# A one-layer token tower: row maxima split and loaded by half the heads, one pipeline step fewer, GpSimd held in three places

## The chip, the cores and the metric

An engine's name in the profile is PE (TensorE), PEld (its weight loads), DVE (VectorE), ACT (ScalarE), POOL (GpSimd) and SP (SyncE, which issues nearly all DMAs here).

## The reference

32 sequences of 512 tokens go through one layer of width 128, in float32:

```python
h = tok_ref(x)                        # pos + nest[nesting] + seg[segments], times W
h = h + attn_ref(layernorm(h))        # 8 heads of 16, softmax over 512 keys
h = h + ffn_ref(layernorm(h))         # 4 experts: relu(x fc1) loA loB fc2, weighted by a gate

scores = einsum('bshc,bthc->bhst', q, k) * factor
attn = softmax(scores, axis=-1)
ctx = einsum('bhst,bthc->bshc', attn, v)
```

The softmax needs the maximum of each row of scores, of which a sequence has 8 heads x 512 rows.

## The kernel before

The program is a software pipeline written out by hand. A step `t` has 16 slots; in it every engine works on several sequences at once, each at another stage: the token embedding of sequence t+4, the queries and keys of t+4 and their pieces of t+3, the row maxima of t+1 and t+2, the attention of t, the output and gate of t-2, the experts' end of t-3. The tables `PRODUCTS`, `ACT_WORK`, `DVE_WORK`, `POOL_WORK` and `SP_WORK` say what each engine does in which slot, and for which sequence; every engine runs its list in order, so an instruction that waits for a semaphore holds up all behind it. SP's and GpSimd's lists have no slots, only an order.

**Scores twice.** Queries and keys are cut into three bfloat16 pieces by GpSimd ("second", "residual", "third"), stored by SP to a DRAM tensor (`stack_dram`, six DMAs) and read back as stacks of 96 rows, `qstk` and `kstk` (three DMAs each, "stack"). One score product per head and 128 queries, [queries, keys] in the bank `mix`, only serves VectorE's row maximum (`row_max`, 32 a sequence). The second, transposed, [keys, queries] in the ring `sc` of three banks, is exponentiated by ScalarE (`exp`, 32 a sequence); it has 24 further rows, in which the negative maxima, again as three pieces for each of 8 heads, are multiplied by ones of the right head and so subtracted. Before, the 32 maxima of a sequence are cut into pieces at once (`cut_max`, four VectorE operations), turned by four products (`turn_max`), copied by one ScalarE copy (`copy_mT`), and one DMA (`load_max`) spreads them over the stack of all heads.

**One step.** Each slot has two maximum products, one product of another stage (`PRODUCTS`) and two score products; behind every fourth slot stand the value products `pv` (16 records). Maxima of a sequence run from slot `MSTART` = 10 of a step to slot 9 of the next, two steps ahead of its exponentials, which fill slots 0 to 15 of step t. `mix` has four banks that take turns: the second maximum of a slot reuses the bank of the other product of the slot before. The exponentials' sums come out of the value products; SP stores them, loads them back spread out, VectorE inverts them (`invert_den`, slot 7), SP stores and loads the inverses, and GpSimd multiplies (`normalise`).

**The order on SP** in a step, before: the six piece stores with the denominators' DMAs between them, ids, the output, inverses, rstd, the maxima's load, weights, and at the end the six stack loads of sequence t+3.

**The start and end.** Steps run from -5 to 34. In step -2, slot 10, the first maxima start; the first exponentials are in step 0, slot 0; step 31 has the last, and steps 32 to 34 drain.

```python
MSTART = 10
return t + (2 if c >= MSTART else 1), (s_max, TILES, 2 * ((c - MSTART) % SLOTS) + kind // 2 + 1)
```

Of the kernel before, what the change touches and what calls it, by code (L numbers as in the profile page):

```python
# [24 lines left out]
ALU = mybir.AluOpType  # L25
# [16 lines left out]
KROWS = STK + 3 * NH  # L42
# [3 lines left out]
MSTART = 10  # L46
RING, MIX = 3, 4
U = 4
HB, H2 = 5, 2
# [5 lines left out]
    ("project", -2), ("fc1_3", -3), ("embed", 4), ("low", -3), ("none", None), ("xn2T", -2), ("out", -3), ("gates", -2),  # L55
    ("turn_gates", -2), ("fc1_0", -2), ("fc1_1", -2), ("mT", 1), ("q", 4), ("fc1_2", -2), ("k", 4), ("v", 4),
# [4 lines left out]
BEFORE, BEHIND = (3, 7), (11,)  # L61

ACT_WORK = [
    (1, 1, "relu", -3, 3), (4, 0, "qk", 3, 0), (4, 0, "qk", 3, 1), (4, 0, "ctx", -1, 1), (6, 0, "xn2T", -2, 0),
    (8, 0, "gates", -2, 0), (9, 1, "gate_exp", -2, 0), (9, 1, "relu", -2, 0), (10, 1, "relu", -2, 1),
    (12, 0, "rT", 4, 0), (12, 0, "wT", -2, 0), (12, 0, "mT", 1, 0), (12, 1, "ctx", 0, 0), (13, 1, "relu", -2, 2),
    (15, 2, "v", 4, 0),
# [40 lines left out]
def tower(nc, x, posT, catT, consts, ident, tokW, qkvT, qkb, bv, ob, woT, wo_q, gateT, fc1T, loA, loBT, fc2T, out):  # L108
# [7 lines left out]
    with ExitStack() as ctx:  # L116
# [60 lines left out]
        onehot = sb("onehot", [HOT, S], BF16)  # L177
# [11 lines left out]
        vals = sb("vals", [P, U, NT, NH, Q])  # L189
# [81 lines left out]
        s_mTmm, s_mT, s_mrow = sem("s_mTmm"), sem("s_mT"), sem("s_mrow")  # L271
# [45 lines left out]
        def _(sp):  # L317
# [883 lines left out]
```

## Time and profile before

| | us |
|---|---|
| three timed runs | 1127.64, 1130.84 (median), 1141.0 |
| the profiled execution | 1126.86 |
| its span, first to last instruction | 1125.1 |
| mean granted clock | 0.962 |

In a row of the timeline the columns are start, length, engine, line, operation, result<-operands, shapes, count, and in brackets how long the engine stood idle before it and for what. In the rows of stretches each engine has its busy time and, in brackets, its number of instructions. Matmuls overlap in the timeline; the chain of waits counts each once. Starts are us from the first instruction.

### The profile page before, as it was taken

The numbers are of one execution on the slowest core, as the hardware profiler recorded it, in microseconds if no ns is written. First come the engines' busy times: TensorE is split into PE (matmuls) and PEld (weight loads), VectorE is DVE, ScalarE is ACT, GpSimd is POOL, SyncE is SP. The second block draws the span as 40 slices with busy tenths as digits, with TensorE's granted clock in tenths as the row PEclk, the third lists the DMA queues.
The fourth block names the chain that finished last, engine by engine and source line by source line (L and its number), as shares of the span: only waits on it lengthen the run. The fifth ranks groups of instructions, "written<-read, shape, count | busy, mean of one in ns | idle before, by whom it ended". The sixth has DMA issues, their size and how long they took to land.

```text
span 1125.1 us, 20263 instructions
## 1 busy us (share of the span) xinstructions
PE 1040.1 (92%) x6158; PEld 407.9 (36%) x6158; DVE 948.8 (84%) x2442; ACT 807.0 (72%) x1578; POOL 682.1 (61%) x684
## 2 busy tenths in 40 slices
PE   4368999999999999999999999999999999989865
PEld 2112233333434434343433443434343343333322
DVE  7498899999989989899999999999999998887312
ACT  2217787777877788787877778778787777856731
POOL 1855676677666666677666666667766666621231
PEclk9558999999999999999999999999999999999997
DMA  2553645555554445555555545565555554541111
GB/s 74 148 135 89 137 106 135 129 137 127 137 130 124 126 121 130 142 127 134 126 137 126 126 121 132 130 143 126 137 125 137 128 126 113 121 96 36 55 50 32
DMA packets 93530, 132.43 MB, mean 118 GB/s; under 512 B 18205, under 2 KB 69918, under 8 KB 87398
## 3 DMA queue, kind: packets, MB, share of 16 engines
q1 hardware_dynamic: 91872, 129.54, 47.9%
q10 hardware_dynamic: 1550, 1.59, 0.6%
q8 instruction: 50, 0.82, 0.3%
q14 instruction: 58, 0.48, 0.1%
HBM read 89.20 MB, written 35.01 MB: 110 GB/s over the span
## 4 chain that ended last, share of the span: by engine, by line
PE 64%; DVE 16%; DMA 6%; ACT 5%; issue 2%; POOL 1%; SPq 1%; POOLq 0%; ACTq 0%; DVEq 0%
PE pv L737 17%; PE mix L750 15%; PE sc L724 13%; DVE negmax L1025 9%; PE mix L804 7%; DMA den_dram<-ctx_sb 4%; PE mix L787 3%; DVE bn L1015 2%; ACT probs L592 2%; PE mix L809 2%; DVE h L1050 2%; PE mix L825 2%; DMA den<-den_dram 2%; ACT qk L596 1%; PE mix L769 1%
## 5 line engine op out<-in xcount | busy, mean ns | idle before, releaser
L1025 DVE TENSOR_REDUCE negmax<-mix 128x1 f32<-128x512 f32 x1024 | 649.0, 679 | 56.8 <-PE mix L750 56.2
L592 ACT ACTIVATE probs<-sc 128x512 f32<-128x512 f32 x1024 | 556.3, 600 | 118.2 <-PE sc L724 112.0
L724 PE MATMUL sc<-qstk,kstk 120*128 120x512 bf16 x1024 | 364.2, 382 | 5.6 <-ACT probs L592 4.9
L750 PE MATMUL mix<-kstk,qstk 96*128 96x512 bf16 x1024 | 331.7, 395 | 24.6 <-DMA kstk<-stack_dram 7.3
L737 PE MATMUL pv<-probs,vals 128*32 128x512 f32 x2048 | 244.8, 595 | 0.0
L528 POOL TENSOR_TENSOR ctxh<-ctx_sb,rdenb 128x512 f32<-128x512 f32 x64 | 81.0, 1268 | 245.3 <-DMA rdenb<-rden_dram 244.5
L750 PEld LDWEIGHTS mix<-kstk,qstk 96*128 96x128 bf16 x1024 | 89.4, 98 | 266.5 <-DVE negmax L1025 76.1
L724 PEld LDWEIGHTS sc<-qstk,kstk 120*128 120x128 bf16 x1024 | 100.1, 98 | 107.5 <-ACT probs L592 33.4
L804 PE MATMUL mix<-xn2T,fc1T_sb 128*128 128x512 f32 x256 | 138.2, 622 | 0.7 <-ACT hid L646 0.7
L508 POOL TENSOR_TENSOR qk<-qk,rstdb 128x512 f32<-128x512 f32 x64 | 81.1, 1269 | 57.9 <-DMA rstdb<-rstd_dram 53.4
L737 PEld LDWEIGHTS pv<-probs,vals 128*32 128x32 f32 x2048 | 59.1, 109 | 117.4 <-issue 100.1
L646 ACT ACTIVATE hid<-mix 128x512 f32<-128x512 f32 x128 | 76.5, 598 | 31.2 <-PE mix L804 28.7
L502 POOL TENSOR_TENSOR pieces<-qkr,pieces 128x512 bf16<-128x512 f32 x64 | 74.0, 1156 | 8.5
L485 POOL TENSOR_TENSOR pieces<-qk,pieces 128x512 bf16<-128x512 f32 x64 | 74.0, 1156 | 6.6 <-ACT pieces L600 6.6
L479 POOL TENSOR_TENSOR qkr<-qk,pieces 128x512 f32<-128x512 f32 x64 | 74.1, 1159 | 0.0
L460 POOL TENSOR_TENSOR rstd<-ve,minus_half 128x4 f32<-128x4 f32 x64 | 64.9, 1013 | 5.0
L458 POOL TENSOR_TENSOR ve<-mv,eps_sb 128x4 f32<-128x4 f32 x64 | 12.9, 201 | 73.8 <-DVE mv L1021 71.1
L804 PEld LDWEIGHTS mix<-xn2T,fc1T_sb 128*128 128x128 f32 x256 | 43.9, 191 | 36.7 <-DVE negmax L1025 24.7
L605 ACT COPY v<-mix 128x512 f32<-128x512 f32 x32 | 18.8, 586 | 46.8 <-POOL vals L520 39.1
L474 POOL TENSOR_TENSOR hb_sb<-h_sb,obias 128x512 f32<-128x512 f32 x32 | 40.5, 1265 | 15.0 <-DVE h L1050 14.8
L1010 DVE TENSOR_TENSOR qk<-mix,posQK 128x512 f32<-128x512 f32 x64 | 43.4, 679 | 7.1 <-POOL qkr L479 6.6
L1050 DVE TENSOR_TENSOR h<-mix,hb_sb 128x512 f32<-128x512 f32 x32 | 22.1, 692 | 28.6 <-PE mix L787 27.5
(141 smaller groups left out, 1088.5 us busy)
## 6 DMA issues: line engine op xcount, KB each, us to landing
stack_dram<-pieces SPq DMA_DIRECT2D x192, 128.0 KB
rdenb<-rden_dram SPq DMA_DIRECT2D x64, 256.0 KB
qstk<-stack_dram SPq DMA_DIRECT2D x31, 384.0 KB, 6.6
kstk<-stack_dram SPq DMA_DIRECT2D x31, 384.0 KB, 8.8
rstdb<-rstd_dram SPq DMA_DIRECT2D x32, 256.0 KB, 3.4
wrow<-w_dram SPq DMA_DIRECT2D x32, 256.0 KB
out<-out_sb SPq DMA_DIRECT2D x32, 256.0 KB, 2.6
qstk<-stack_dram SPq DMA_DIRECT2D x31, 256.0 KB, 7.0
```

The lines of the kernel that those rows point to most:

```text
L479: pool.tensor_tensor(qkr[:, side, :], qk32[:, side, :], pieces[:, side, 0, :], ALU.subtract).then_inc(s_res0, 1)
L485: pool.tensor_tensor(pieces[:, side, 1, :], qk32[:, side, :], pieces[:, side, 0, :], ALU.subtract).then_inc(s_pc1, 1)
L502: pool.tensor_tensor(pieces[:, side, 2, :], qkr[:, side, :], pieces[:, side, 1, :], ALU.subtract).then_inc(s_pc2, 1)
L508: pool.tensor_tensor(qk32[:, side, :], qk32[:, side, :], rstdb[:], ALU.mult).then_inc(s_scaled, 1)
L528: pool.tensor_tensor(ctxh[:, g, :], ctx_sb[:, u % 2, g, :], rdenb[:, g, :], ALU.mult).then_inc(s_ctxh, 1)
L592: act.activation(probs[:, c % 8, i % 2], sc[:, i % RING], ACT.Exp).then_inc(s_exp, 1)
L646: act.activation(hid[:, e, :], aux(f"fc1_{e}", 1), ACT.Relu).then_inc(s_hid, 1)
L724: pe.matmul(sc[:, i % RING, :], kstk[0:KROWS, u, h, j * P:(j + 1) * P], qstk[0:KROWS, u, h, :], start=True, stop=True).then_inc(s_score, 1)
L737: mm = pe.matmul(pv[Q * i:Q * i + Q, :], vals[:, u, 2 * half + jj, 4 * g + i, :], probs[:, 4 * (r % 2) + i, jj, :], start=(half == 0 and j ...
L750: pe.matmul(max_bank(m), qstk[0:STK, u, h, j * P:(j + 1) * P], kstk[0:STK, u, h, :], start=True, stop=True).then_inc(s_mxmm, 1)
L804: pe.matmul(aux(f"fc1_{e}", 1), fc1T_sb[:, e, :], xn2T[:], start=True, stop=True).then_inc(s_fc1mm, 1)
L1025: dve.tensor_reduce(negmax[:, m // NT, m % NT:m % NT + 1], max_bank(m), AX.X, ALU.max, negate=True).then_inc(s_max, 1)
```

## The change

The maxima are handled by halves, of four heads each. The pieces of a half take 12 rows (`MROWS`), since the same 12 rows serve both halves of the heads, so a score product has 108 rows. `cut_max`, `turn_max`, `copy_mT` and `load_max` exist once for each half: four VectorE operations, four products, four small copies and one DMA each. The maxima of a sequence run from slot 7 of the step before to slot 6 of its own, one step ahead; its exponentials from slot 3 (`SSTART`) of its own to slot 2 of the next. The first half is cut in slot 15 (after 16 maxima) and wanted at slot 3, the second is cut in slot 7 and wanted at slot 11. So everything ahead of it moves one step closer: steps run from -4, stacks have three buffers instead of four, embeddings are three steps ahead instead of four. The v products move from slot 15 to slot 4, the turns of weights and rstd keep slot 11, and VectorE's comparison of ids (`hot`) goes from slot 15 to slot 11, into two buffers.

On SP the first half's load and then the six stack loads of the next sequence stand at the start of a step, the second half's load behind the inverses' stores. GpSimd gets three more waits: before the scaling of queries it waits for the first half's cut, before rstd1 (which now stands before the keys' second piece) for the second half's cut, and before `normalise` for the gate and the ids.

```diff
-KROWS = STK + 3 * NH
+MROWS = 3 * NH // 2
+KROWS = STK + MROWS
-MSTART = 10
+SSTART, MSTART = 3, 7
-U = 4
-HB, H2 = 5, 2
+U, UV = 3, 4
+HB, H2 = 4, 2
...
 DVE_WORK = [
...
+    (6, 1, "moments1", 3, 0), (7, 1, "cut", 0, 1), (7, 1, "finish", -3, 0), (7, 1, "invert_den", -1, 0),
...
+    (13, 0, "add_qk", 3, 0), (15, 1, "cut", 1, 0), (15, 1, "add_qk", 3, 1),
...
 SP_WORK = [
+    ("max_in", 0, 0), ("stack", 1, 0), ("stack", 1, 1),
...
-            def load_max(b, u):
-                upto(sp, s_mT, b)
-                sp.dma_start(qstk[STK:KROWS, u, :, :],
-                             mT[:].unsqueeze(1).broadcast_to([3 * NH, NH, S])).then_inc(s_mrow, 16)
+            def load_max(b, g, u):
+                upto(sp, s_mT, b, 8, 4 * g + 4)
+                sp.dma_start(qstk[STK:KROWS, u, 4 * g:4 * g + 4, :],
+                             mT[:, g].unsqueeze(1).broadcast_to([MROWS, 4, S])).then_inc(s_mrow[g], 16)
...
             def rstd_first(b):
+                upto(pool, s_mp, b - 3, 8, 8)
...
             def scale(b, side):
+                if side == 0:
+                    upto(pool, s_mp, b - 2, 8, 4)
...
+            def normalise(b):
+
+                if b < NSEQ - 1:
+                    upto(pool, s_gate, b - 1, 13)
+                    upto(pool, s_hot, b + 5)
...
-                act.copy(mT[:], aux("mT", 1)[0:3 * NH]).then_inc(s_mT, 1)
...
+                for j in range(NT):
+                    act.copy(mT[:, g, j * P:(j + 1) * P], bank[Q * j:Q * j + MROWS, g * P:g * P + P]).then_inc(s_mT, 1)
...
-                if i == 0:
-                    upto(pe, s_mrow, b, 16)
+                if i % 16 == 0:
+                    upto(pe, s_mrow[g], b, 16)
...
+            def second_half(t):
+
+                if runs(t - 2):
+                    upto(pe, s_gat, t - 2)
+                else:
+                    mix_free(t, 3 * 7 + 1)
+                turn_max(t, 1)
```

SP where one step ends and the next begins, before. `qstk<-mT` is the maxima's load, `qstk<-stack_dram` and `kstk<-stack_dram` the stacks:

```order
L379 DMA qstk<-mT 24x8x512 [waits s_mT]
L375 DMA w_dram<-turned 4x4x128 [waits s_win,s_wT]
L412 DMA rstdb<-rstd_dram 128x512 [waits s_rstdout,s_scaled]
L417 DMA wrow<-w_dram 128x1x512 [waits s_wout,s_low]
L356 DMA qstk<-stack_dram 48x1x4096 [waits s_score,s_pcoutq]
L356 DMA qstk<-stack_dram 32x1x4096
L356 DMA qstk<-stack_dram 16x4096
L363 DMA kstk<-stack_dram 48x4096 [waits s_score,s_pcoutk]
L363 DMA kstk<-stack_dram 32x1x4096
L363 DMA kstk<-stack_dram 16x4096
L339 DMA stack_dram<-pieces 8x16x512 [waits s_stkq,s_pc0]
L339 DMA stack_dram<-pieces 8x16x512 [waits s_stkk,s_pc0]
```

and now:

```order
L376 DMA w_dram<-turned 4x4x128 [waits s_win,s_wT]
L413 DMA rstdb<-rstd_dram 128x512 [waits s_rstdout,s_scaled]
L418 DMA wrow<-w_dram 128x1x512 [waits s_wout,s_low]
L380 DMA qstk<-mT 12x4x512 [waits s_mT]
L357 DMA qstk<-stack_dram 48x1x4096 [waits s_score,s_pcoutq]
L357 DMA qstk<-stack_dram 32x1x4096
L357 DMA qstk<-stack_dram 16x4096
L364 DMA kstk<-stack_dram 48x4096 [waits s_score,s_pcoutk]
L364 DMA kstk<-stack_dram 32x1x4096
L364 DMA kstk<-stack_dram 16x4096
L340 DMA stack_dram<-pieces 8x16x512 [waits s_stkq,s_pc0]
L340 DMA stack_dram<-pieces 8x16x512 [waits s_stkk,s_pc0]
```

The half's load stands between the weights' load and the stacks, so the stacks wait behind it for ScalarE's copies (`s_mT`).

SP in the middle of a step, before. `stack_dram<-pieces` that waits for `s_pc1` is a second piece, `rden_dram<-rden` the inverses' stores, `rdenb` their load:

```order
L422 DMA out<-out_sb 128x4x128 [waits s_out]
L339 DMA stack_dram<-pieces 8x16x512 [waits s_pc1]
L392 DMA rden_dram<-rden 4x16x32 [waits s_rden,s_rdin1,s_rdin0]
L392 DMA rden_dram<-rden 4x16x32
L339 DMA stack_dram<-pieces 8x16x512 [waits s_pc2]
L400 DMA rdenb<-rden_dram 128x1x512 [waits s_rdout,s_ctxh]
L400 DMA rdenb<-rden_dram 128x1x512 [waits s_ctxh]
```

and now:

```order
L423 DMA out<-out_sb 128x4x128 [waits s_out]
L340 DMA stack_dram<-pieces 8x16x512 [waits s_pc1]
L393 DMA rden_dram<-rden 4x16x32 [waits s_rden,s_rdin1,s_rdin0]
L393 DMA rden_dram<-rden 4x16x32
L380 DMA qstk<-mT 12x4x512 [waits s_mT]
L401 DMA rdenb<-rden_dram 128x1x512 [waits s_rdout,s_ctxh]
L401 DMA rdenb<-rden_dram 128x1x512 [waits s_ctxh]
L340 DMA stack_dram<-pieces 8x16x512 [waits s_pc2]
```

The second half's load stands behind the second piece and the inverses' stores, and before the inverses' load; the third piece (`s_pc2`) moved behind that.

GpSimd in the middle of a step, before. `ve` and `rstd` are rstd1's two operations, `pieces<-qk,pieces` a second piece, `qkr` the residual, `pieces<-qkr,pieces` the third piece:

```order
L485 TENSOR_TENSOR pieces<-qk,pieces 128x512 [waits s_pcoutq,s_pc0]
L479 TENSOR_TENSOR qkr<-qk,pieces 128x512 [waits s_pc0]
L502 TENSOR_TENSOR pieces<-qkr,pieces 128x512 [waits s_pcoutq,s_res0,s_pc1]
L485 TENSOR_TENSOR pieces<-qk,pieces 128x512 [waits s_pcoutk,s_pc0]
L458 TENSOR_TENSOR ve<-mv,eps_sb 128x4 [waits s_mv1,s_rTmm,s_v]
L460 TENSOR_TENSOR rstd<-ve,minus_half 128x4 [waits s_ve1]
L479 TENSOR_TENSOR qkr<-qk,pieces 128x512 [waits s_pc0]
L502 TENSOR_TENSOR pieces<-qkr,pieces 128x512 [waits s_pcoutk,s_res0,s_pc1]
L528 TENSOR_TENSOR ctxh<-ctx_sb,rdenb 128x512 [waits s_rdin0]
```

and now:

```order
L487 TENSOR_TENSOR pieces<-qk,pieces 128x512 [waits s_pcoutq,s_pc0]
L481 TENSOR_TENSOR qkr<-qk,pieces 128x512 [waits s_pc0]
L504 TENSOR_TENSOR pieces<-qkr,pieces 128x512 [waits s_pcoutq,s_res0,s_pc1]
L459 TENSOR_TENSOR ve<-mv,eps_sb 128x4 [waits s_rTmm,s_mv1,s_v,s_mp]
L461 TENSOR_TENSOR rstd<-ve,minus_half 128x4 [waits s_ve1]
L487 TENSOR_TENSOR pieces<-qk,pieces 128x512 [waits s_pcoutk,s_pc0]
L481 TENSOR_TENSOR qkr<-qk,pieces 128x512 [waits s_pc0]
L504 TENSOR_TENSOR pieces<-qkr,pieces 128x512 [waits s_pcoutk,s_res0,s_pc1]
L535 TENSOR_TENSOR ctxh<-ctx_sb,rdenb 128x512 [waits s_rdin0,s_hot,s_gate]
```

rstd1 moved in front of the keys' second piece and waits for `s_mp`, the second half's cut; the multiplication by the inverses waits for `s_gate` and `s_hot` as well.

TensorE in slot 7, before. `mix<-kstk,qstk` is a maximum product, `sc` a score product, `mix<-xn2T,gateT_sb` the gate, `pv` the values:

```order
L750 MATMUL mix<-kstk,qstk 128x512 [waits s_xn2T]
L750 MATMUL mix<-kstk,qstk 128x512 [waits s_max]
L724 MATMUL sc<-qstk,kstk 128x512 [waits s_exp] x2
L794 MATMUL mix<-xn2T,gateT_sb 32x128 [waits s_xn2T,s_max]
L794 MATMUL mix<-xn2T,gateT_sb 32x128 x3
L737 MATMUL pv<-probs,vals 32x512 [waits s_ctx,s_exp,s_v]
L737 MATMUL pv<-probs,vals 32x512 x7
L750 MATMUL mix<-kstk,qstk 128x512 [waits s_out]
L750 MATMUL mix<-kstk,qstk 128x512 [waits s_max]
```

and now:

```order
L763 MATMUL mix<-kstk,qstk 128x512 [waits s_xn2T]
L763 MATMUL mix<-kstk,qstk 128x512 [waits s_stkk,s_stkq,s_max]
L737 MATMUL sc<-qstk,kstk 128x512 [waits s_exp] x2
L811 MATMUL mix<-xn2T,gateT_sb 32x128 [waits s_xn2T,s_max]
L811 MATMUL mix<-xn2T,gateT_sb 32x128 x3
L750 MATMUL pv<-probs,vals 32x512 [waits s_ctx,s_exp,s_v]
L750 MATMUL pv<-probs,vals 32x512 x7
L797 MATMUL mix<-id,mpc 12x128 [waits s_mp,s_gat]
L797 MATMUL mix<-id,mpc 12x128 x3
L763 MATMUL mix<-kstk,qstk 128x512 [waits s_out]
L763 MATMUL mix<-kstk,qstk 128x512 [waits s_max]
```

The first maximum product of the slot is now the first of a new sequence and waits for both stacks (`s_stkk`, `s_stkq`); the second half's turn stands behind the values.

## Rows read from the trace of the kernel before

**Rows 1.** Busy times by stretch (us, busy and instruction count by engine, PEclk, DMA share, GB/s).

```profile
49.71:85.83 36.12, 26.11 (x70) 6.19 (x69) 34.48 (x65) 4.94 (x10) 24.24 (x25) 0.50 0.61 143
501.97:533.63 31.66, 31.22 (x193) 12.31 (x192) 28.72 (x76) 25.05 (x50) 21.20 (x21) 1.00 0.54 130
815.02:846.21 31.19, 31.05 (x193) 12.35 (x192) 28.70 (x76) 24.92 (x50) 21.24 (x21) 1.00 0.53 126
1044.43:1070.39 25.96, 23.56 (x144) 9.19 (x144) 5.71 (x26) 20.63 (x43) 6.61 (x8) 1.00 0.17 51
```

**Rows 2.** The chain of waits, 815 to 850 us: start, length, what.

```profile
820.78 0.09 PE mix L780 x2
...
826.18 0.28 PE mix L774 x4
...
826.68 1.85 PE pv L737 x16
...
841.53 0.43 PE mix L750 x2
...
844.47 0.54 PE mix L750 x2
...
845.55 0.43 PE mix L750 x2
...
849.68 0.43 PE sc L724 x2
```

**Rows 3.** ScalarE's timeline in the fill.

```profile
25.05 3.60 ACT L581 CAST kstk<-const_sb 24x4096 bf16<-24x4096 f32 x1
```

**Rows 4.** ScalarE's timeline of a steady step.

```profile
821.45 0.26 ACT L636 COPY turned<-mix 16x128 f32<-16x128 f32 x1
```

**Rows 5.** SP's timeline of the same step.

```profile
823.89 0.87 SPq L379 DMA_DIRECT2D qstk<-mT  x1
...
827.95 1.87 SPq L356 DMA_DIRECT2D qstk<-stack_dram  x3
829.92 1.58 SPq L363 DMA_DIRECT2D kstk<-stack_dram  x3
...
838.56 0.52 SPq L369 DMA_DIRECT2D den_dram<-ctx_sb  x1
...
842.39 0.34 SPq L385 DMA_DIRECT2D den<-den_dram  x1
...
845.08 0.59 SPq L339 DMA_DIRECT2D stack_dram<-pieces  x1
845.78 1.11 SPq L392 DMA_DIRECT2D rden_dram<-rden  x2
```

**Rows 6.** DMA issues, 815 to 847 us: KB each, median us to landing.

```profile
kstk<-stack_dram SPq DMA_DIRECT2D x1, 128.0 KB, 10.1
ids_b<-ids_dram SPq DMA_DIRECT2D x1, 64.0 KB, 2.6
...
den<-den_dram SPq DMA_DIRECT2D x1, 16.0 KB, 1.8
```

**Rows 7.** DMA issues in the fill, 56 to 86 us.

```profile
kstk<-stack_dram SPq DMA_DIRECT2D x2, 128.0 KB, 8.3
```

**Rows 8.** GpSimd's timeline of the steady step.

```profile
821.01 2.52 POOL L528 TENSOR_TENSOR ctxh<-ctx_sb,rdenb 128x512 f32<-128x512 f32 x2 [6.33 <-DMA rdenb<-rden_dram]
...
840.90 1.16 POOL L485 TENSOR_TENSOR pieces<-qk,pieces 128x512 bf16<-128x512 f32 x1
...
843.42 1.16 POOL L479 TENSOR_TENSOR qkr<-qk,pieces 128x512 f32<-128x512 f32 x1
```

**Rows 9.** VectorE's timeline of the steady step.

```profile
817.31 0.19 DVE L1033 CAST mpc<-negmax 128x32 bf16<-128x32 f32 x1
...
818.11 0.68 DVE L1025 TENSOR_REDUCE negmax<-mix 128x1 f32<-128x512 f32 x1
```

**Rows 10.** VectorE's timeline in the fill.

```profile
73.73 0.95 DVE L1033 CAST mpc<-negmax 128x32 bf16<-128x32 f32 x1
```

More of the change, by code:

```diff
@@ L81 @@
-    ("residual", 3, 1), ("third", 3, 1), ("normalise", -1, 0), ("v", 3, 0),
+    ("scale", 2, 0), ("add_bias", 2, 0), ("scale", 2, 1), ("rstd2", -2, 0), ("norm2", -2, 0),
+    ("second", 2, 0), ("residual", 2, 0), ("third", 2, 0), ("rstd1", 3, 0), ("second", 2, 1),
+    ("residual", 2, 1), ("third", 2, 1), ("normalise", -1, 0), ("v", 3, 0),
 ]
 SP_WORK = [
-    ("piece", 3, (0, 0)), ("piece", 3, (1, 0)), ("den_out", -1, 1), ("piece", 3, (0, 1)), ("den_in", -1, 0),
-    ("piece", 3, (0, 2)), ("ids", 5, 0), ("out", -3, 0), ("piece", 3, (1, 1)), ("rden_out", -1, 0), ("piece", 3, (1, 2)),
@@ L86 @@
-    ("rden_in", -1, 0), ("rstd_out", 4, 0), ("den_out", 0, 0), ("max_in", 1, 0), ("weights_out", -2, 0),
-    ("rstd_in", 4, 0), ("weights_in", -2, 0), ("stack", 3, 0), ("stack", 3, 1),
+    ("max_in", 0, 0), ("stack", 1, 0), ("stack", 1, 1),
+    ("piece", 2, (0, 0)), ("piece", 2, (1, 0)), ("den_out", -1, 1), ("piece", 2, (0, 1)), ("den_in", -1, 0),
+    ("piece", 2, (0, 2)), ("ids", 4, 0), ("out", -3, 0), ("piece", 2, (1, 1)), ("rden_out", -1, 0), ("max_in", 0, 1),
+    ("rden_in", -1, 0), ("piece", 2, (1, 2)), ("rstd_out", 3, 0), ("den_out", 0, 0), ("weights_out", -2, 0),
@@ L309, in steps @@
         def steps(eng, step):
-            for t in range(-5, NSEQ + 3):
+            for t in range(-4, NSEQ + 3):
                 step(t, t % U)
@@ L451, in _ @@
         def _(pool):
-            for v in range(U):
+            for v in range(UV):
                 pool.memset(vals[:, v, :, 0:4, HC:Q], 1.0).then_inc(s_pconst, 1)
@@ L635, in copy_wT @@
                 upto(act, s_wout, b - 1, 16 * WREP)
-                act.copy(wT, aux("mT", 1)[Q:Q + NT * NE, 0:P]).then_inc(s_wT, 1)
+                act.copy(wT, aux("turned", 1)[Q:Q + NT * NE, 0:P]).then_inc(s_wT, 1)
             def copy_rT(b):
@@ L662, in step @@
                 for c in range(SLOTS):
-                    if t == -4 and c == 13:
+                    if t == -3 and c == 13:
                         fill_heads()
+                    if t == -3 and c == 4:
+                        copy_rT(0)
                     for place in range(3):
                         for name, ahead, part in [w[2:] for w in ACT_WORK if w[:2] == (c, place)]:
-                            if runs(t + ahead):
+                            if runs(t + ahead) and not (name == "rT" and t == -3):
                                 work[name](t + ahead, (u + ahead) % U, part)
-                        if place < 2 and runs(t):
-                            exp(t, 2 * c + place)
+                        b = t if c >= SSTART else t - 1
+                        if place < 2 and runs(b):
+                            exp(b, 2 * ((c - SSTART) % SLOTS) + place)
             steps(act, step)
@@ L850, in mix_user @@
                     name, ahead = PRODUCTS[c]
-                    if name == "none":
-                        return -1, (s_h, 1, 1)
-                    if name == "mT" and not runs(t + 1):
-                        return (t - 2, (s_wT, 1, 1)) if t > 0 else (t + 4, (s_rT, 1, 1))
+                    if name == "turned":
+                        return (t - 2, (s_wT, 1, 1)) if runs(t - 2) else (t + 3, (s_rT, 1, 1))
+                    if name == "gates" and runs(t):
+                        return t, (s_mT, 8, 8)
                     return t + ahead, products[name][1]
-                return t + (2 if c >= MSTART else 1), (s_max, TILES, 2 * ((c - MSTART) % SLOTS) + kind // 2 + 1)
+                return t + (1 if c >= MSTART else 0), (s_max, TILES, 2 * ((c - MSTART) % SLOTS) + kind // 2 + 1)
             def mix_free(t, n):
@@ L866, in row_tile @@
             def row_tile(t, u, c, i):
-                ahead = 2 if c >= MSTART else 1
+                ahead = 1 if c >= MSTART else 0
                 if runs(t + ahead):
@@ L1106, in tile_max @@
             def tile_max(t, c, i):
-                ahead = 2 if c >= MSTART else 1
+                ahead = 1 if c >= MSTART else 0
                 if runs(t + ahead):
```

181 lines of the change are left out of this document (90 added, 91 removed).

## The prediction, made before the changed kernel ran

> **What bounds the kernel now.** I read the busy times by stretch first, then the chain of waits through one step, then the four other engines' timelines of the same step. In a steady step TensorE is busy 31.05 us of 31.19 at the full 2.4 GHz (granted clock 1.00), VectorE 28.70, ScalarE 24.92, GpSimd 21.24 [rows 1]. A faster neighbour buys almost nothing there: 0.14 us a step. The chain of waits says the same: it is mostly TensorE's own products, one behind the other, from one group of value products to the next [rows 2]. Two stretches are different. Before the first exponential, VectorE's maxima run alone: 36.12 us for 22 slots, 1.64 us a slot, TensorE at granted clock 0.50 (its lower level, 1.2 GHz) [rows 1]. And in the last step with exponentials, which has no maxima, the step takes 25.96 us instead of 31.19 [rows 1], so a slot with maxima costs 0.33 us more than one without.
>
> The profiled execution took 1126.86 us, its span 1125.1, so 1.8 lie around it; the median of the three timed runs is 1130.84. I sum against 1126.86. A difference of about 2% (1108 to 1153 about the median) is what a measurement of this kernel can tell from none.
>
> **The change part by part.** *One pipeline step less.* The maxima of a sequence now start 12 slots before its exponentials, not 22, and the exponentials start at slot 3 of their step. From the first maximum to the start of step 0 it was 22 slots and is 9: 13 x 1.64 = 21.3 us less. Against it: the maxima now also fill step 31 up to slot 6, 13 slots more at 0.33 = 4.3 us. Step 32 gets 6 score products, 6 x 0.22 = 1.3 us (two took 0.43 in the chain [rows 2]). And in the fill ScalarE's head rows (3.60 us [rows 3]), which were written while ScalarE waited, now stand in front of the first query copy: 0 to 3.6, I take 2. Together 21.3 - 4.3 - 1.3 - 2 = 13.7 us gained once.
>
> *TensorE's own work.* Score products have 108 rows instead of 120 but the same 512 columns, so I cost them at nothing. The turn of the maxima becomes 8 products for 4; two took 0.09 us in the chain [rows 2], so +0.18 a step. The v products (0.28 [rows 2]) only move, from slot 15 to slot 4. The value products now follow their exponentials by less than a slot, not by four: in front of those of slot 11 ScalarE will just be finishing. That wait lies beside the load of slot 11 (below), so it costs nothing of its own; without that cover it is about 0.3.
>
> *The stack loads move behind the half's load; the first cover to go.* Let S be the end of the value products in slot 15, 826.68 + 1.85 = 828.53 [rows 2]. The turn takes 0.18, then ScalarE makes four copies; the nearest row is its 16x128 copy, 0.26 [rows 4], so 1.1 with the gaps: 829.9. Then SP issues the half's load (the whole one held SP 0.87 [rows 5]) and only then the six stack loads: 830.4 to 830.8 where the first started at 827.95 [rows 5], so 2.7 later. They were wanted a step later; now slot 7 of the same step wants them all. The last of the six was issued at about 829.92 + 1.58 - 0.6 = 830.9 and landed after 10.1 us [rows 5, 6], at 841.0. Shifted it lands at 843.7; if it lands after 8.3, as in the fill [rows 7], at 841.9. TensorE reaches slot 7's first maximum at 841.53 + 0.22 = 841.75 [rows 2], plus 0.18 for the turn and 0.28 for v: 842.2. So it waits 0 to 1.5 us. Ahead of the loads there is less in the queue than now, but more than in the fill; I take 0.8, the middle. Behind the waiting product stand that slot's scores, gates and values, and everything after.
>
> *The second half.* It is cut in slot 7, turned behind slot 7's values and wanted in slot 11. The turn ends 0.18 after 844.47 [rows 2], the four copies 1.1 after that, 845.8; the second maximum of slot 8 reuses that bank and stood at 845.55 [rows 2], 845.7 with the turn. With semaphores 0 to 0.4, I take 0.2.
>
> *GpSimd held.* "rstd1" now stands ahead of the keys' second piece and waits for the second half's cut. Before, the piece starts at 840.90, rstd1 follows it, and the next piece starts at 843.42 [rows 8]: 2.5 us for the two. Count from T, the start of slot 7's first maximum: product 0.4, maximum 0.68, cut 0.80 (817.31 to 818.11 [rows 9]), so the cut is done at T + 1.9; rstd1 and the piece 2.5, a semaphore 0.1: T + 4.5. For GpSimd this is hidden: it sits idle 6.33 us a step for the denominators anyway [rows 8], and the second hold (gate and ids, in slot 11) ends about when those land. But SP stands in order: the store of this piece, the two denominator stores, and then the second half's load. From 845.08 to 845.78 and 1.11 more [rows 5] is 1.8, so the load starts at T + 6.3. A 64 KB load lands after 2.6 us and a 16 KB one after 1.8 [rows 6]; this one has 48 KB. It lands at T + 8.1 to 8.9, and later if it queues behind the output's store. TensorE wants it at 849.68 - 841.75 = 7.93 [rows 2], plus 0.18 and 0.2: T + 8.3. A wait of 0 to 1.3; I take 0.5.
>
> What the hold buys is the cut itself. In steady steps a cut's first operation takes 0.19 us [rows 9]; with GpSimd busy beside it, in the fill, one took 0.95 [rows 10]. The Trainium skill (SBUF — State Buffer, "Who interferes with whom") says why: VectorE's second port pair and GpSimd's are one, locked for a whole instruction. By that rule the new cut of slot 7, unheld, would lose up to one GpSimd operation, and the hold is worth about 0.8 a step; the trace of the fill agrees with 0.95 against 0.19, but in steady steps of before there is no such loss to win back. My sum has the cut at 0.80 and needs no sentence of this.
>
> *Sum.* Per step 0.18 + 0.8 + 0.2 + 0.5 = 1.68; bounds 0.18 and 0.18 + 1.5 + 0.4 + 1.3 = 3.4. 31 steps have all of it: 52 us (6 to 105). 1126.9 - 13.7 + 52 = **1165**. VectorE's four extra operations (about 0.2 each), ScalarE's eight small copies (8 x 0.26) and the moved v copy lie in those engines' spare 2.5 and 6.3 us.
>
> **Rivals.** *Everything lands in time.* The stack loads take the fill's 8.3 us and the half's load 1.8, so TensorE never waits: 1126.9 - 13.7 + 6 = 1119. For it: a load slower than the fill's has always had other loads ahead of it. Against: 841.9 against 842.2 leaves 0.3 us of room, and only if nothing is late. It decides once the last stack load lands within 11.5 us of the first one's issue.
>
> *The denominators come late too.* Their store was issued at 838.56, behind the stack loads, and the load back only at 842.39 [rows 5]: 3.8 us. With the stacks 2.7 us later VectorE may wait for them in slot 7, where its maxima queue behind, for another 1 us: 1165 + 31 = 1196. The Trainium skill (DMA: Bandwidth & Descriptors, "Queues, rings and completion order") says that each DMA engine takes its descriptors in the order of the ring; by that rule the store must wait for all of the stacks' descriptors on its engines, and the 3.8 us agree. Against this rival: VectorE itself reaches that point 1.5 us later, since the cut and the output's sum now stand in front.
>
> *The steady step gets shorter.* Some steps took 31.66 instead of 31.19 [rows 1]; if that is VectorE waiting for denominators, later demand ends it, and if the loads land as well it is 1119 - 10, about 1108. Nothing else in the rows could give: TensorE has no more than 0.14 us a step to win.
>
> **How the numbers follow.** Waits as summed 0.55, with its own range 1140 to 1190; all in time 0.25; denominators late as well 0.15; steady step shorter 0.05. Below 1108: 0.05 of the last and 0.02 of the second, 0.07. Above 1153: 0.42 of the forecast and 0.15, 0.57. Within 2%: 0.36. The range 1112 to 1196 leaves out about 0.05 below and 0.08 above.
>
> **What would show it.** Right: the first exponential near 70 us instead of 85.8 [rows 1]; steady steps of about 32.9 us; TensorE waiting each step for the stack load at the first maximum of slot 7 and for the maxima's load at the first score of slot 11, with SP's piece store behind GpSimd just before. Wrong: steps of 31.4 or less, or the waits elsewhere, say at slot 3 for the first half. Steps over 34 us, with VectorE's reciprocal waiting for the denominators, would be the second rival.

## The result, and the profile after

The changed kernel takes 1177.16 us (median of 4 runs, 1173.64 to 1178.84) where the kernel before took 1129.24 us beside it: ratio 1.040, 95% interval 1.032 to 1.049. It is slower. The profiled execution took 1178.84 us, its span 1177.0.

First the length of a step. VectorE compares the ids once in each step, so the time from the first to the last start of that group, divided by one less than its count, is the mean step: before (921.4 - 264.0) / 21 = 31.30 us, after (921.0 - 254.5) / 20 = 33.33. The row is from the view of one tile, 250 to 950 us: count, ns least/median/most, first and last start. Of before:

```profile
L996 DVE TENSOR_SCALAR onehot<-ids_b,const_sb x22: 332/382/857, 264.0 to 921.4; 96x512 bf16<-96x512 bf16 x22
```

Of after, with the exponentials of the whole span, whose first start fell from 85.8 [rows 1] to 70.7:

```profile
L1021 DVE TENSOR_SCALAR onehot<-ids_b,const_sb x21: 338/340/342, 254.5 to 921.0; 96x512 bf16<-96x512 bf16 x21
...
L599 ACT ACTIVATE probs<-sc x1024: 589/597/699, 70.7 to 1130.4; 128x512 f32<-128x512 f32 x171
```

So 15.1 us are gained at the start, and 2.03 a step are lost: 31 x 2.03 = 63. Behind the last exponential 3.5 us are gained (1177.0 - 1130.4 = 46.6; before 1125.1 - 1075.0 = 50.1, by the same view). The spans differ by 51.9, so another 7.5 us are lost; they lie in the steps that fill and empty the pipeline, since the steady steps and both ends are counted.

Busy times by stretch of after, the fill from the first maximum to the first exponential and one steady step, which answer to [rows 1]:

```profile
52.77:70.68 17.91, 14.29 (x38) 3.09 (x36) 17.00 (x32) 1.29 (x6) 11.53 (x12) 0.50 0.34 92
827.22:860.24 33.02, 31.24 (x196) 12.63 (x195) 29.90 (x80) 26.30 (x57) 20.94 (x22) 1.00 0.49 120
```

TensorE is still busy 31.24 us and at granted clock 1.00, but now 1.8 us of the step are idle. The four groups of value products cut the step into four parts, which shows where. Before, TensorE's timeline:

```profile
826.61 1.92 PE L737 MATMUL pv<-probs,vals 128*32 128x512 f32 x16
...
835.29 1.90 PE L737 MATMUL pv<-probs,vals 128*32 128x512 f32 x16
...
842.57 1.90 PE L737 MATMUL pv<-probs,vals 128*32 128x512 f32 x16
...
850.04 1.92 PE L737 MATMUL pv<-probs,vals 128*32 128x512 f32 x16
...
857.79 1.92 PE L737 MATMUL pv<-probs,vals 128*32 128x512 f32 x16
```

After, the same, with the only idle times over 0.15 us in the step, which are all that this view shows (in brackets, with what ended them):

```profile
827.22 1.92 PE L750 MATMUL pv<-probs,vals 128*32 128x512 f32 x16
...
829.46 0.23 PE L797 MATMUL mix<-id,mpc 128*12 128x128 bf16 x4 [0.32 <-DVE mpc L1065]
829.99 0.60 PE L763 MATMUL mix<-kstk,qstk 96*128 96x512 bf16 x2 [0.30 <-DVE qk L1035]
...
836.81 1.90 PE L750 MATMUL pv<-probs,vals 128*32 128x512 f32 x16
...
844.43 1.90 PE L750 MATMUL pv<-probs,vals 128*32 128x512 f32 x16
...
847.09 0.38 PE L737 MATMUL sc<-qstk,kstk 108*128 108x512 bf16 x1
847.61 0.61 PE L763 MATMUL mix<-kstk,qstk 96*128 96x512 bf16 x2
...
852.59 0.60 PE L737 MATMUL sc<-qstk,kstk 108*128 108x512 bf16 x2 [0.91 <-DMA qstk<-mT]
853.12 1.92 PE L750 MATMUL pv<-probs,vals 128*32 128x512 f32 x16
...
860.24 1.92 PE L750 MATMUL pv<-probs,vals 128*32 128x512 f32 x16
```

| part of the step | before | after | difference |
|---|---|---|---|
| values of slot 15 to slot 3 | 8.68 | 9.59 | +0.91 |
| slot 3 to 7 | 7.28 | 7.62 | +0.34 |
| slot 7 to 11 | 7.47 | 8.69 | +1.22 |
| slot 11 to 15 | 7.75 | 7.12 | -0.63 |

The last part only lost work: the turn (behind slot 11 before) and the v products, which now stand in slot 4. The second part grew mostly by those v products. So the losses lie in two places, slot 15 and slot 11, with a smaller one in slot 8. Slot 7's stack load, where the prediction put its largest term, is small. TensorE's waits of after, 250 to 950 us (total, times, longest), some 21 steps:

```profile
PE sc L737 <- DMA qstk<-mT: 17.0, 20, 2.0
PE mix L797 <- DVE mpc L1065: 7.8, 19, 0.6
PE mix L763 <- DVE qk L1035: 6.2, 21, 0.3
PE mix L763 <- DMA kstk<-stack_dram: 2.1, 7, 0.5
```

Of the same stretch, a wait of TensorE's weight loads:

```profile
PEld mix L763 <- ACT mT L620: 10.3, 21, 0.5
```

*Slot 8.* The slot's second maximum product starts 0.52 us behind the score product before it (847.09 to 847.61), where it was 0.22 (845.17 to 845.39). It reuses the bank from which ScalarE copies the second half, and the last of those copies ends at 847.56 (below). This loss of 0.30 is in no bracket, because it falls into gaps under 0.15.

*Slot 11.* SP's timeline of that step:

```profile
831.79 2.33 SPq L357 DMA_DIRECT2D qstk<-stack_dram  x3
...
848.14 0.59 SPq L340 DMA_DIRECT2D stack_dram<-pieces  x1
848.85 1.11 SPq L393 DMA_DIRECT2D rden_dram<-rden  x2
850.00 0.87 SPq L380 DMA_DIRECT2D qstk<-mT  x1
```

GpSimd's, of both places:

```profile
827.66 1.18 POOL L524 TENSOR_TENSOR vals<-v,rstd 128x256 f32<-128x256 f32 x2
...
845.70 0.20 POOL L459 TENSOR_TENSOR ve<-mv,eps_sb 128x4 f32<-128x4 f32 x1 [3.25 <-DVE mpc L1065]
...
846.96 1.15 POOL L487 TENSOR_TENSOR pieces<-qk,pieces 128x512 bf16<-128x512 f32 x1
```

and ScalarE's four copies of the second half:

```profile
846.46 1.10 ACT L620 CAST mT<-mix 12x128 bf16<-12x128 f32 x4 [1.14 <-PE mix L797]
```

The half was ready at 847.56 and its load went out at 850.00, 2.4 us later. In between SP stood at the store of a piece, which GpSimd finished at 848.11 because it had been held to 845.70, and then issued that store and the two of the inverses, 1.8 us.

*Slot 15.* VectorE's two cuts (first and second half):

```profile
827.99 0.32 DVE L1059 CAST mpc<-negmax 128x16 bf16<-128x16 f32 x1
828.34 0.55 DVE L1061 TENSOR_TENSOR mres<-negmax,mpc 128x16 f32<-128x16 f32 x1
...
844.81 0.17 DVE L1059 CAST mpc<-negmax 128x16 bf16<-128x16 f32 x1
845.01 0.19 DVE L1061 TENSOR_TENSOR mres<-negmax,mpc 128x16 f32<-128x16 f32 x1
```

The held cut of slot 7 has 0.17 and 0.19. In slot 15 GpSimd's values (827.66 to 828.84) run beside it; the hold that is meant for this cut stands on the scaling of the queries, one place behind the values in GpSimd's order, so the values are free to run into the cut.

### The profile page after: what moved, and what is told of

Read it like the earlier page. It is cut to its first block and busy times, and to the rows that moved or that the text cites. A ratio compares the mean times of both kernels' runs of the same rounds, so it can differ in the third digit from the quotient of the medians.

```text
span 1177.0 us, 21121 instructions
## 1 busy us (share of the span) xinstructions
PE 1049.2 (89%) x6286; PEld 416.8 (35%) x6286; DVE 975.2 (83%) x2570; ACT 852.0 (72%) x1802; POOL 681.7 (58%) x684
## 5 line engine op out<-in xcount | busy, mean ns | idle before, releaser
L599 ACT ACTIVATE probs<-sc 128x512 f32<-128x512 f32 x1024 | 562.6, 605 | 78.9 <-PE sc L737 72.7
L737 PE MATMUL sc<-qstk,kstk 108*128 108x512 bf16 x1024 | 369.1, 384 | 26.4 <-DMA qstk<-mT 24.4
L763 PE MATMUL mix<-kstk,qstk 96*128 96x512 bf16 x1024 | 325.2, 390 | 42.6 <-DVE qk L1035 11.5
L750 PE MATMUL pv<-probs,vals 128*32 128x512 f32 x2048 | 250.8, 608 | 1.4 <-ACT probs L599 0.9
L763 PEld LDWEIGHTS mix<-kstk,qstk 96*128 96x128 bf16 x1024 | 83.2, 98 | 246.5 <-DVE negmax L1050 67.5
L737 PEld LDWEIGHTS sc<-qstk,kstk 108*128 108x128 bf16 x1024 | 97.6, 98 | 148.3 <-ACT probs L599 43.9
L620 ACT CAST mT<-mix 12x128 bf16<-12x128 f32 x256 | 65.7, 257 | 100.1 <-PE mix L797 95.4
L518 POOL TENSOR_TENSOR v<-v,posV 128x512 f32<-128x512 f32 x32 | 40.7, 1273 | 3.9 <-ACT v L612 3.9
```

What stands on the lines that cost most here:

```text
L599: act.activation(probs[:, c % 8, i % 2], sc[:, i % RING], ACT.Exp).then_inc(s_exp, 1)
L737: pe.matmul(sc[:, i % RING, :], kstk[0:KROWS, u, h, j * P:(j + 1) * P], qstk[0:KROWS, u, h, :], start=True, stop=True).then_inc(s_score, 1)
L750: mm = pe.matmul(pv[Q * i:Q * i + Q, :], vals[:, b % UV, 2 * half + jj, 4 * g + i, :], probs[:, 4 * (r % 2) + i, jj, :], start=(half == 0 ...
L763: pe.matmul(max_bank(m), qstk[0:STK, u, h, j * P:(j + 1) * P], kstk[0:STK, u, h, :], start=True, stop=True).then_inc(s_mxmm, 1)
```

## The experiments

All are edits of the changed kernel. "Step" is worked out as above; "cut" and "half's load" are how long TensorE waited, between 250 and 950 us, for VectorE's cut and for the maxima's load, counting waits over 0.15 us.

| run | median us | ratio to before, interval | step | cut (times) | half's load (times) |
|---|---|---|---|---|---|
| the changed kernel | 1177.16 | 1.040, 1.032 to 1.049 | 33.33 | 7.8 (19) | 17.0 (20) |
| e1_rstd1_free | 1197.68 | 1.061, 1.058 to 1.064 | 34.24 | 33.7 (40) | 0.5 (1) |
| e2_half_load_first | 1177.61 | 1.044, 1.040 to 1.047 | 33.66 | 28.6 (21) | none |
| e3_v_in_front | 1163.87 | 1.030, 1.027 to 1.033 | 32.94 | 0.3 (1) | 20.1 (21) |
| e4_both | 1147.99 | 1.017, 1.014 to 1.019 | 32.34 | 9.1 (22) | none |
| e5_v_free | 1149.94 | 1.017, 1.015 to 1.020 | 32.35 | none | none |
| e6_rden_first | 1148.00 | 1.016, 1.014 to 1.018 | 32.36 | none | none |
| e7_no_holds | 1231.39 | 1.090, 1.087 to 1.093 | 34.96 | 41.0 (37) | none |
| e8_stacks_first | 1411.45 | 1.250, 1.245 to 1.255 | 41.3 | 5.4 (12) | 117.5 (33) |
| e12_vals_after_gate | 1137.48 | 1.008, 1.005 to 1.010 | 32.0 | none | none |
| e13_cut_first | 1133.61 | 1.004, 1.002 to 1.006 | 31.80 | none | none |
| e14_den_later | 1145.14 | 1.014, 1.011 to 1.018 | 32.13 | none | 11.0 (22) |
| e15_q_stack_early | 1220.55 | 1.081, 1.078 to 1.085 | 35.6 | none | 51.3 (19) |

**One hold off.**

```diff
 def rstd_first(b):
-    upto(pool, s_mp, b - 3, 8, 8)
     upto(pool, s_v, b - 2, 2)
```

> The changed kernel, with one of its holds taken away: GpSimd's rstd1 no longer waits for the second half's cut; its place in the order and the other holds stay. Theory (the wait of slot 11 is made by this hold: SP's piece store stands behind the held GpSimd work and the second half's load behind that store): the wait at the first score of slot 11 (0.91 us in the step read, 38.5 us over 29 steps) shrinks to under 0.3, and the cut of slot 7 grows from 0.73 us, by up to the 0.6 that the unheld cut of slot 15 has more. Net per step -0.3 to -0.9 us, so 1150 to 1170 us. Rival (the load of slot 11 is late because the second half itself is late: maxima, cut, turn, four copies): the wait stays and the time is 1177 or, with the longer cut in front of it, 1177 + 30 x 0.5 = 1192.

The wait of slot 11 went, as the theory had it, so this hold does make it. But the cut that it had protected cost far more than 0.6:

```profile
L1062 DVE CAST mpc<-mres x41: 174/525/1116, 249.9 to 934.4; 128x16 bf16<-128x16 f32 x41
```

An operation of 0.174 took up to 1.116, and TensorE waited for the cut 33.7 us. In the cut read (831.29 to 833.95) not one but two of the four operations were stretched, to 1.12 and 1.08. The time came out above both numbers: the place of the wait was right, the price of an unheld cut was not.

**SP's order alone.** The second half's load is moved in front of the piece store.

```diff
-    ("out", -3, 0), ("piece", 2, (1, 1)), ("rden_out", -1, 0), ("max_in", 0, 1),
+    ("out", -3, 0), ("max_in", 0, 1), ("piece", 2, (1, 1)), ("rden_out", -1, 0),
```

> The changed kernel, with the second half's load moved on SP in front of the keys' piece store and the store of the reciprocals, so that it no longer stands behind GpSimd's held work. Theory (SP's order makes the wait of slot 11): the four copies were done at 847.56 and the load was issued at 850.00, 2.4 us later; issued at once the wait of 0.91 is gone, 30 steps x 0.9 to 1.3 us = 27 to 39 us less, 1138 to 1150 us. Rival 1 (the denominators' reciprocals, now behind this load, become what is waited for): 1165 to 1177. Rival 2 (VectorE, 83% busy, is the bound behind the wait, and the wait only moves): 1172 to 1180.

The wait of slot 11 is gone and nothing is won. The reciprocals now go out later, so GpSimd's normalising and the values run later, straight into the cut of slot 15 (in the step read the normalising's addition runs from 831.25 to 832.53 and the values' from 832.49, and the cut starts at 832.09). TensorE waited for the cut 28.6 us instead of 7.8:

```profile
L1059 DVE CAST mpc<-negmax x41: 160/172/1306, 261.0 to 934.0; 128x16 bf16<-128x16 f32 x41
```

The time is that of rival 2, but not for its reason: what moved was GpSimd's timing, and e4 below, which shelters this cut too, does win.

**GpSimd's order alone, and both.** The values go in front of the normalising and get its hold.

```diff
-    ("third", 2, 1), ("normalise", -1, 0), ("v", 3, 0),
+    ("third", 2, 1), ("v", 3, 0), ("normalise", -1, 0),
...
 def value(b):
+    if b >= 2:
+        upto(pool, s_gate, b - 5, 13)
+        upto(pool, s_hot, b + 1)
```

> The changed kernel, with GpSimd's values (v) in front of normalise instead of behind it, and the hold that normalise has (gate and ids) put on v as well, so that v does not run beside the first half's cut. Theory (the cut of slot 15 is stretched from 0.73 to 1.29 us because GpSimd works beside it, and TensorE waits for it at the turn): the cut of slot 15 takes 0.7 to 0.9, the wait at the turn of slot 15 shrinks by 0.4 to 0.6, so 30 x 0.4 to 0.6 = 12 to 18 us less, 1159 to 1165 us. Rival (the cut is late because its last maximum is late, the turn follows too closely whatever GpSimd does): the cut is shorter but TensorE waits the same, 1174 to 1180; or normalise, now behind v, delays the projection and the time rises.

> Both edits at once: the second half's load in front on SP, and GpSimd's values in front of normalise with the hold. Theory (two separate waits, slot 11 and slot 15): the gains add, 1177 - (27 to 39) - (12 to 18) = 1120 to 1138 us. Rival (both waits are one lateness of VectorE seen in two places): as the better of the two alone.

The first, e3, came out as its theory had it: the wait for the cut fell from 7.8 us to 0.3, and 1177.2 - 1163.9 = 13.3 us were won. Both together won 29: with the cut out of the way, SP's order, worth nothing alone, is worth 16. That is less than the sum that the theory gave (1120 to 1138) and more than the better edit alone, its rival, since the held values push the normalising into the cut again. GpSimd:

```profile
837.35 2.50 POOL L538 TENSOR_TENSOR ctxh<-ctx_sb,rdenb 128x512 f32<-128x512 f32 x2
839.93 1.28 POOL L542 TENSOR_TENSOR ctxn<-ctxh 128x512 f32<-128x512 f32 x1
```

VectorE:

```profile
840.46 0.78 DVE L1062 CAST mpc<-negmax 128x16 bf16<-128x16 f32 x1
```

The cast that started at 840.46 ends at 841.24, with GpSimd's addition (to 841.21).

**Which holds the values need.** From both edits: first the hold on the values taken away again; then, on SP, the store of the reciprocals in front of the half's load, its load behind it and the pieces last; then a hold for the gate alone on the two scalings.

> The kernel of the run before (second half's load in front on SP, values in front of normalise on GpSimd), with the hold on the values taken away again; normalise keeps its own. Theory (a cut costs TensorE what GpSimd works beside it): in the run before the held values began at 834.86, normalise ended at 841.2 and the cut of slot 15 began at 840.46, with 0.78 us for a first operation of 0.16; with the values beside the gate instead, normalise ends some 2 us before the cut, the cut takes 0.8 instead of 1.35, 30 steps x 0.5 = 15 us less: 1130 to 1136 us. Rival (the values now stretch the gate, which has some ten small operations, and the hidden layers wait): the gate grows by 1 us or more, 1148 to 1165 us.

> As the run before this one, and on SP the store of the reciprocals in front of the second half's load, their load behind it, and both piece stores last. Theory: nothing waits for the reciprocals' load once the values stand in front of normalise, and the second half's load goes out 1.1 us later but has about 2 us of room, so no change: within 5 us of the run before this one. Rival (normalise still waits for the reciprocals in some steps: 54.9 us in 10 of them): 5 to 10 us less.

```diff
     upto(pool, s_rstd1, b)
+    if b >= 2:
+        upto(pool, s_gate, b - 5, 13)
     upto(pool, s_pv, b - UV, 8)
```

> The kernel of the run with the reciprocals' store first (1148.0 us), with a hold of GpSimd's two scalings of the values, and of these alone, until the gate of the same step is through; the addition in front of them stays free. Theory (the gate's products with gsm and gad took 0.37 and 0.47 us beside the values there, 0.175 each where the values waited, and TensorE's turn of the gates behind slot 11 waits for them; the cut of slot 15 stays clear because normalise ends at about 874.0 where it began at 874.5): gsm and gad at 0.175, cut at 0.75, and 0.5 us a step less: 1148 - 15 = 1133 us. Rival (normalise is pushed into the cut of slot 15, as in the run with everything held): cut at 1.1 to 1.35, time 1145 to 1150.

Without the hold (e5) the cut was short in every step and the time still the same, so the loss had moved to the gate, as the rival of e5 had it. Groups of VectorE by line in e5, x count | busy, mean ns:

```profile
L1100 DVE SCALAR_TENSOR_TENSOR gad<-grec,gsm 128x16 f32<-128x16 f32 x32 | 14.7, 458 | 1.1
L1097 DVE TENSOR_TENSOR gsm<-lexp,grec 128x16 f32<-128x16 f32 x32 | 11.6, 361 | 1.1
```

With the narrow hold of e12 the same two:

```profile
L1099 DVE TENSOR_TENSOR gsm<-lexp,grec 128x16 f32<-128x16 f32 x32 | 5.6, 175 | 1.1
L1102 DVE SCALAR_TENSOR_TENSOR gad<-grec,gsm 128x16 f32<-128x16 f32 x32 | 5.6, 175 | 1.1
```

Two operations are 0.47 us a step shorter, and the time fell by 10.5 us from e6 (theory 15). The reciprocals' place on SP (e6) was worth nothing that these runs can tell: 1148.0 against 1149.9, as its theory had it.

**All holds off, and the order of the stacks.**

> The changed kernel with all of GpSimd's holds taken away (for the maxima's halves, the gate and the ids); its order stays. Theory (GpSimd beside VectorE's small operations stretches them, 1.9 us for the cut of slot 7 when its hold alone was taken): both cuts at 2 to 2.6 us, the gate longer too; some 1195 to 1215 us. Rival (only the one hold mattered, and the others cost as much as they save): 1190 to 1200, as with the one hold taken away (1197.7).

> The changed kernel with the six stack loads in front of the first half's load on SP again. Theory (the first half is wanted at slot 3, some 6 us after its turn, so six loads in front of it make TensorE wait there, and slot 7 wins back its 0.27): the load is issued 3.5 us later, ends behind 768 KB of stacks, and the first score of slot 3 waits 1 to 4 us a step: 1205 to 1290 us. Rival (the half's load was in time by more than 3.5 us, and the order is worth nothing): 1169 to 1177 us.

Without holds the kernel loses another 54 us: they are worth that much in this order, more than the theory had (1195 to 1215), and the rival is refuted. With the six stack loads in front, the first half's load makes TensorE wait at slot 3. SP:

```profile
919.99 1.60 SPq L364 DMA_DIRECT2D kstk<-stack_dram  x3
921.75 0.89 SPq L380 DMA_DIRECT2D qstk<-mT  x1
```

TensorE:

```profile
931.75 1.03 PE L737 MATMUL sc<-qstk,kstk 108*128 108x512 bf16 x2 [5.42 <-DMA qstk<-mT]
```

Issued at 921.75, the 48 KB let TensorE go at 931.75, ten us later. By the view of DMA issues the six loads ahead of it are 1536 KB, not the 768 of the expectation, and the last of them landed 10.5 us after its issue. The theory's mechanism is shown; its 1 to 4 us a step were 8 (41.3 against 33.3). Of these, 5.4 are the wait itself in the step read. Nearly all of the rest is TensorE's clock. Behind the wait (us, busy and count by engine, PEclk, DMA share, GB/s):

```profile
931.75:935.00 3.25, 3.25 (x14) 0.72 (x18) 0.28 (x1) 2.57 (x5) 0.18 (x1) 0.50 0.02 5
```

TensorE had stood idle for 5.4 us and came back at granted clock 0.50, its lower level: from that product to the first maximum product behind slot 3's values (937.71) it took 5.96 us, where the changed kernel took 3.37 (835.28 to 838.65), so 2.6 more. Slot 11's wait is about what it was in the changed kernel, 1.0 against 0.9.

**Three attempts at the rest.** In e13, the cut and the sum behind it go from place (15, 1) to (15, 0) of VectorE's table, in front of the slot's first maximum; in e14, the denominators' reciprocals also go from (7, 1) to (8, 1); in e15, without that, the next sequence's query stacks go behind the reciprocals' load on SP.

> As the run before this one, and VectorE's cut of the first half and the sum of the keys' product in front of slot 15's first maximum instead of behind it. Theory (TensorE waits 0.28 us a step at slot 0's first maximum for the bank that this sum frees, and the cut itself ends just when the turn is due): both end 0.6 us earlier, the wait goes, 30 x 0.28 = 8 us less than the run before. Rival (VectorE has no slack there and the maxima of slot 15, 1.4 us later, take the wait over): no change, within 4 us.

> As the run before this one, and VectorE's reciprocals of the denominators one slot later (slot 8). Theory (VectorE waits for the denominators' load in about half of the steps, 11.5 us in 14 of them in the run with the reciprocals' store first, and stands 93% busy): 5 to 10 us less than the run before. Rival (the wait lies in VectorE's slack; the later reciprocals only push normalise towards the cut of slot 15): no change, or up to 10 us more.

> The kernel of the run with the cut in front of slot 15's maxima (1133.6 us), with the three query stack loads of the next sequence issued on SP some 11 us earlier, behind the load of the reciprocals in the step before, and only the three key loads left behind the first half's load. Theory (what is left of slot 7 is the last stack load: TensorE waits for it 7.0 us in 14 of 22 steps, 0.62 in the step read, and VectorE 10.1 us for the denominators that stand behind the loads on SP): the key loads go out 2 us earlier and alone, the wait of slot 7 goes, 30 x 0.3 = 10 us less, 1120 to 1127 us, just under the kernel before. Rival (384 KB more beside the loads of rstd and of the weights make GpSimd's first scaling late, which sets the pieces and so the key loads): 1133 to 1150 us.

The first took TensorE's wait for the bank away (6.0 us in 22 steps) and 3.9 us of time, half of its theory's 8 and within its rival's 4: the wait for the stacks in slot 7 grew from 3.8 to 7.0. The intervals of e12 and e13 just overlap (1.005 to 1.010, 1.002 to 1.006), so that gain is likely, not shown. The second lost 11.5 us, for a reason that neither its theory nor its rival had: SP stands at the later reciprocals' store, with the half's load behind it, and slot 11 waits again (11.0 us in 22 steps). The third lost 87 us, more than its rival had and at another place. SP:

```profile
846.63 1.85 SPq L357 DMA_DIRECT2D qstk<-stack_dram  x3
...
850.65 0.25 SPq L408 DMA_DIRECT2D rstd_dram<-turned  x1
...
856.93 0.35 SPq L413 DMA_DIRECT2D rstdb<-rstd_dram  x1
857.58 0.58 SPq L418 DMA_DIRECT2D wrow<-w_dram  x1
858.82 0.83 SPq L380 DMA_DIRECT2D qstk<-mT  x1
```

The load of rstd waits for its 2 KB store, 6.3 us behind it instead of 3.2 in e13 (852.03 to 855.26 there). It and the weights' load then go out just in front of the first half's, 512 KB ahead of 48, and slot 3 waits 51.3 us in 19 steps. Here too TensorE came back at granted clock 0.50 (866.74 to 869.41, behind a wait of 3.73).

No version beat the kernel before. The best, e13, is at 1.004: the same by the 2% named ahead, though its interval (1.002 to 1.006) lies just above one. Its first exponential comes at 69.5 us, so it keeps the start that was won; its step is still 0.50 longer than before, which over 31 steps is 15.5 us and eats it.

## Why the prediction was right, point by point

*The outcome.* Forecast 1165 within 1112 to 1196, slower; measured 1177. The losses per step were forecast at 1.68 and were 2.03, the single gain at 13.7 and was 11 (15.1 + 3.5 - 7.5). That the losses came so close is in part luck: slot 7's term was 0.7 too large, and slot 15's, which was missing, measured 0.7. By the prediction's own signs, the first exponential, the step and slot 11 came about as said; TensorE's wait in slot 7 came in 7 of 21 steps and not in each, and a wait "elsewhere", its sign of being wrong, came in slot 15.

*The single gain.* The first exponential came at 70.7 as forecast. From the first maximum to it there are now 12 slots, 7 to 15 and 0 to 2, which took 17.91 us, 1.49 a slot where it was 1.64. The first maximum comes 3.1 us later (52.77 against 49.71), for which the prediction took 2, as ScalarE's head rows in front of the first query copy. What its product waited for was another thing, the copy of v:

```profile
52.12 3.03 PE L763 MATMUL mix<-kstk,qstk 96*128 96x512 bf16 x6 [9.37 <-ACT v L612]
```

The end behind the last exponential, 3.5 shorter, was not in the sum. The 7.5 lost in filling and emptying answer to its 4.3 and 1.3, and no run separates them.

*Slot 7, forecast 0.8, measured 0.1* (2.1 us in 21 steps). This term was the largest and the most wrong. The loads do go out later, 4.6 us behind the start of slot 15's values (827.22 to 831.79) where it was 1.3 (826.61 to 827.95 [rows 5]), 3.2 us for the 2.7 forecast; but the last one lands sooner. After, landing of the third key load:

```profile
kstk<-stack_dram SPq DMA_DIRECT2D x2, 128.0 KB, 8.4
```

It is 8.4 us, the fill's 8.3 [rows 7], not the 10.1 of before [rows 6]. The bound stated for this case was the right one; the middle of the range was not. Part of the 0.1 may be cover, as TensorE already waited in slot 15: in e13, without those waits, slot 7 costs 0.32 (7.0 us in 22 steps).

*Slot 11, forecast 0.5, measured 0.8* (17.0 us in 21 steps; 0.91 in the step shown). The mechanism is the one predicted: the piece store behind held GpSimd, with e1 and e2 each taking the wait away from its own side. The load was issued 2.4 us after the half was ready.

*Slot 15, no term in the sum, measured 0.7* (7.8 and 6.2 us in 21 steps; 0.32 and 0.30 in the step shown). This is the step of the prediction that failed: S was taken as the end of the value products, "the turn takes 0.18", as if TensorE found the cut ready, with the cut at 0.80. But the cut has its last maximum only one slot before and stands behind slot 15's first maximum; its hold stands behind the values, so they run beside it, and then the maxima's bank comes free 0.30 late too. e3, which clears this cut alone, won 13.3 us, 0.43 a step; in e13 the wait for the bank is gone.

*Slot 8's bank, forecast 0.2, measured 0.3* in the step shown, by the mechanism that the prediction named: the product starts 0.05 behind the last of the four copies.

*The turns and the moved v.* The second turn was put at 0.18 more. The first product behind slot 7's values starts 1.89 us behind their start (844.43 to 846.32), where it was 1.83 (842.57 to 844.40), so it costs about 0.1. The v products only changed their part of the step, as costed. The terms come to 0.1 + 0.8 + 0.7 + 0.3 + 0.1 = 2.0 of the 2.03.

*The hold of slot 7* stood outside the sum, priced at up to one GpSimd operation, about 0.8 a step. That was too low: in e1 two operations of one cut were stretched one after the other, by 1.85 us together.

*The rivals.* "Everything lands in time" is refuted by the waits of slots 11 and 15, though slot 7 came out nearly its way. "The denominators come late too" is refuted: VectorE waited 8.1 us for them between 250 and 950, where before it was 20.7. "The steady step gets shorter" is refuted: it is 2.03 longer.

*What stays open.* What makes up the last 0.50 us a step of e13. Its wait for the last stack load, 0.32 (7.0 us in 22 steps), and slot 8's bank, 0.3 if it is as in the changed kernel, would more than cover it, so something else has become shorter; no run took either away, since e15 cost more than it could give.

## What to carry to other kernels

A hold keeps back only those instructions of its engine that stand behind it: look at which ones stand in front of it, and whether they can run into the thing to be protected. Where an engine issues in order, ask of each hold which store of which queue stands behind it, since a hold that pays on one engine can cost through the next load: rstd1's hold costs 0.8 us a step in slot 11, and without it the kernel is still 20.5 us slower. An edit that removes a proven wait and wins nothing, like e2, may only have changed when something else runs: repair both places together before judging either.

## What was not expected of the hardware

GpSimd's work does not stretch all of VectorE's, but a few kinds only. In e7, where nothing is held, 250 to 950 us:

```profile
L1053 DVE CAST mpc<-negmax x40: 157/168/1224, 256.1 to 937.3; 128x16 bf16<-128x16 f32 x40
L1055 DVE TENSOR_TENSOR mres<-negmax,mpc x40: 185/190/1150, 256.3 to 937.5; 128x16 f32<-128x16 f32 x40
...
L1044 DVE TENSOR_REDUCE negmax<-mix x643: 656/681/693, 250.4 to 949.7; 128x1 f32<-128x512 f32 x161
```

Casts and two-operand sums in SBUF took up to 1.22 us, about one GpSimd instruction (1.16 to 1.27), and the comparison of ids, 0.34 us, took up to 1.38; the 643 maxima, beside the same work, never took over 0.693. So the small operations of a cut need shelter, and the 0.68 us maxima, two thirds of VectorE's time, need none.

The Trainium skill ("SBUF — State Buffer", section "Who interferes with whom") says that a tensor_reduce never contends on this chip, and that a VectorE operation with two SBUF inputs, or a cast in a two-port mode, can be blocked for a whole GpSimd instruction. The trace agrees on both: 0.693 at most for the one, 1.224 for the other.

On SP's queue, in these two runs, a small transfer took as long as what stood ahead of it. In e15 a 2 KB store behind 768 KB of loads and 256 KB of stores was followed by its load only 6.3 us later instead of 3.2, and in e8 48 KB behind 1536 KB took ten us to release TensorE. A 16 KB load of before landed in 1.8 us [rows 6].
